# Bias of a fused adapter, router and expert layer: partial sums folded to 64 rows with high and low halves in one product, and a ScalarE copy put in another place

## What is computed

```python
# first layer, for tile b with adapter A = lora_As[itok[b]], Bm = lora_Bs[itok[b]]
y = x @ W.T + b1 + 2.0 * (x @ A) @ Bm
# second layer on y
base   = y @ base_w.T + base_b
hidden = y @ A2.T                          # 64 columns
probs  = softmax(y @ router_w.T)           # 16 experts
topw, topi = top_k(probs, 2); topw = topw / (sum(topw) + 1e-6)
delta  = sum over the two experts e of topw[e] * hidden @ B[e].T
out    = x + base + 0.5 * delta
```

## Time and profile before

| | |
|---|---|
| median of 3 runs | 101.2 us (101.11 to 102.17) |
| the profiled execution | 101.23 us |
| its span, first to last instruction | 99.4 us |
| TensorE busy | 95.7 us, 96% of the span |
| VectorE, ScalarE, GpSimd busy | 67%, 42%, 22% |
| chain that ended last | 93% TensorE, 3% transfers, 0% VectorE and ScalarE |

### The profile page before, as it was taken

The page is one execution under the profiler, slowest core; times in us unless marked ns, Lnnn a source line. Parts: engine busy times, 40 slices in busy tenths (PEclk is TensorE's granted clock), DMA queues, the critical chain, the costliest instruction groups (busy, mean ns, idle before and its releaser), DMA issues.

```text
span 99.4 us, 1810 instructions
## 1 busy us (share of the span) xinstructions
PE 95.7 (96%) x572; PEld 87.2 (88%) x572; DVE 66.1 (67%) x183; ACT 41.8 (42%) x102; POOL 22.2 (22%) x34
## 2 busy tenths in 40 slices
PE   6899999999999999999999999999999999999990
PEld 6799999999999999998898799888787887878980
DVE  5669995997475885998977577257949275572101
ACT  3615526968787545756422610451424022040000
POOL 4100004325999965109122000000000000000000
PEclk9999999999999999999999999999999999999999
DMA  2999569899457786882590736416307465020211
GB/s 37 356 364 391 174 125 377 265 366 361 121 91 191 196 257 142 229 233 47 175 300 25 206 127 178 138 35 196 109 20 199 134 170 147 0 105 0 105 59 53
DMA packets 8379, 16.91 MB, mean 170 GB/s; under 512 B 1507, under 2 KB 4067, under 8 KB 8370
## 3 DMA queue, kind: packets, MB, share of 16 engines
q1 hardware_dynamic: 7762, 16.41, 54.5%
q10 hardware_dynamic: 576, 0.39, 1.2%
q0 software_dynamic: 32, 0.00, 0.0%
HBM read 13.28 MB, written 2.16 MB: 155 GB/s over the span
## 4 chain that ended last, share of the span: by engine, by line
PE 93%; DMA 3%; DVE 0%; ACT 0%; issue 0%
PE pair L819 90%; DMA w_raw_all<-w_cat 3%; PE pair L964 1%; PE pair L966 1%; PE pair L984 1%; DVE xn L813 0%; ACT w_hi_all L421 0%; PE pair L954 0%; PE pair L943 0%; PE pair L941 0%; PE pair L933 0%
## 5 line engine op out<-in xcount | busy, mean ns | idle before, releaser
L819 PE MATMUL pair<-e_hi,w_hi_all 128*128 128x512 f32 (+1 forms) x72 | 27.1, 376 | 0.0
L819 PE MATMUL pair<-e_hi,w_lo_all 128*128 128x512 f32 (+1 forms) x72 | 26.7, 370 | 0.0
L819 PE MATMUL pair<-e_lo,w_hi_all 128*128 128x512 f32 (+1 forms) x72 | 26.7, 370 | 0.0
L536 ACT ACTIVATE w_hi_all<-exp_raw_all 128x512 fp32r<-128x512 f32 x16 | 9.7, 630 | 15.3 <-DVE exp_raw_all L754 15.3
L819 PEld LDWEIGHTS pair<-e_hi,w_lo_all 128*128 128x128 f32 x72 | 13.5, 188 | 2.5
L819 PEld LDWEIGHTS pair<-e_hi,w_hi_all 128*128 128x128 f32 x72 | 13.6, 188 | 2.5
L819 PEld LDWEIGHTS pair<-e_lo,w_hi_all 128*128 128x128 f32 x72 | 13.6, 189 | 2.0
L761 DVE TENSOR_TENSOR w_lo_all<-exp_raw_all,w_hi_all 128x512 fp32r<-128x512 f32 x16 | 10.4, 688 | 4.5 <-ACT w_hi_all L536 3.9
L754 DVE TENSOR_TENSOR exp_raw_all<-w_raw_all 128x512 f32<-128x512 f32 x16 | 11.1, 735 | 0.2 <-DMA w_raw_all<-spill 0.2
L768 DVE TENSOR_TENSOR xn<-pair,xn 128x512 f32<-128x512 f32 x7 | 4.8, 690 | 9.1 <-PE pair L819 9.1
L819 PE MATMUL pair<-p_hi,x_hi 128*128 128x304 f32 x32 | 10.0, 311 | 0.0
(11 more groups left out here) (108 smaller groups left out, 162.5 us busy)
## 6 DMA issues: line engine op xcount, KB each, us to landing
w_raw_all<-spill SPq DMA_DIRECT2D x16, 256.0 KB, 4.0
...
```

The costliest lines, as they stand in the source:

```text
L536: nc.scalar.activation(gt_hi[:, t % 2, js, :], g[:, js, :], ACT.Copy).then_inc(gh_done, 1)
L819: return nc.tensor.matmul(out_ap, lhs, rhs, start=first, stop=last)
```

## The change

1. The bias is summed over 64 rows. `bias_up`, 64x592, takes ScalarE's copy of the lower 64 rows of `bias_part`; VectorE adds the upper 64 rows to it. The rounded high part goes to rows 0 to 63 of one tile `bp_split`, the low part to rows 64 to 127, and two matmuls with the ones sum both at once, in place of four.
2. `bias_part_of(2)` moves ahead of `folded_lo(0)` on VectorE. On ScalarE the copy to `bias_up` stands ahead of `c_hi`.
3. The x copy of the third tile (`x_hi_part(2)`) moves ahead of the last `folded_hi`, with waits for its input and for the end of the folding.
4. The low part of the first tile's adapter rows is a VectorE copy from `c_lo` in place of the subtraction from PSUM; it waits for `cl_done` in place of `first_high`. `x_first(1)` no longer waits for `first_low`.

```diff
--- before.py
+++ after.py
@@ -95,8 +95,10 @@
         c_hi = sb("c_hi", [P, W2N], F32R)
         c_lo = sb("c_lo", [P, W2N], F32R)
         bias_part = sb("bias_part", [P, W2N])
-        bp_hi = sb("bp_hi", [P, W2N], F32R)
-        bp_lo = sb("bp_lo", [P, W2N], F32R)
+
+        bias_up = sb("bias_up", [P // 2, W2N])
+
+        bp_split = sb("bp_split", [P, W2N], F32R)
         bias_hi = sb("bias_hi", [FT, W2N], F32R)
         low_row = sb("low_row", [FT, 1])
         c_stack = sb("c_stack", [FT, NT, W2N], F32R)
@@ -207,6 +209,8 @@
         ch_done = sem("ch_done")
         cl_done = sem("cl_done")
         bias_step = sem("bias_step")
+        bias_moved = sem("bias_moved")
+        bias_added = sem("bias_added")
         bph_done = sem("bph_done")
         bpl_done = sem("bpl_done")
         pe_bias = sem("pe_bias")
@@ -458,16 +462,21 @@
             nc.scalar.activation(lb_hi[:, :, :].rearrange("p k (t r) -> p t k r", t=NT),
                                  lora_raw[:, :, KC * R:AL].rearrange("p t (k r) -> p t k r", k=KC),
                                  ACT.Copy).then_inc(lbh_done, 1)
-            for n in range(KC):
+            for n in range(KC - 1):
                 folded_hi(n)
+
             act.wait_ge(in_xt[1], 16)
+            act.wait_ge(pe_p, KC)
             x_hi_part(2)
+            folded_hi(KC - 1)
             x_hi_part(3)
             split_experts(0)
+            act.wait_ge(bias_step, KC)
+            nc.scalar.activation(bias_up[:, :], bias_part[P // 2:, :], ACT.Copy).then_inc(bias_moved, 1)
             act.wait_ge(pe_c, 1)
             nc.scalar.activation(c_hi[:, :], w2_cols(ps_c), ACT.Copy).then_inc(ch_done, 1)
-            act.wait_ge(bias_step, KC)
-            nc.scalar.activation(bp_hi[:, :], bias_part[:, :], ACT.Copy).then_inc(bph_done, 1)
+            act.wait_ge(bias_added, 1)
+            nc.scalar.activation(bp_split[0:P // 2, :], bias_up[:, :], ACT.Copy).then_inc(bph_done, 1)
             def lora_first():
                 z = z_lora[0]
                 act.wait_ge(pe_first, 1)
@@ -655,6 +664,7 @@
             x_lo_early(1)
             bias_part_of(0)
             bias_part_of(1)
+            bias_part_of(2)
             folded_lo(0)
             folded_lo(1)
             dve.wait_ge(lbh_done, 1)
@@ -664,13 +674,15 @@
                                     ALU.subtract).then_inc(lbl_done, 1)
             folded_lo(2)
             folded_lo(3)
-            bias_part_of(2)
             bias_part_of(3)
+            dve.wait_ge(bias_moved, 1)
+            nc.vector.tensor_tensor(bias_up[:, :], bias_part[0:P // 2, :], bias_up[:, :],
+                                    ALU.add).then_inc(bias_added, 1)
             dve.wait_ge(ch_done, 1)
             nc.vector.tensor_tensor(c_lo[:, :], w2_cols(ps_c), c_hi[:, :].bitcast(F32),
                                     ALU.subtract).then_inc(cl_done, 1)
             dve.wait_ge(bph_done, 1)
-            nc.vector.tensor_tensor(bp_lo[:, :], bias_part[:, :], bp_hi[:, :].bitcast(F32),
+            nc.vector.tensor_tensor(bp_split[P // 2:, :], bias_up[:, :], bp_split[0:P // 2, :].bitcast(F32),
                                     ALU.subtract).then_inc(bpl_done, 1)
 
             def lora_first_lo():
@@ -769,9 +781,8 @@
 
             lora_first_lo()
             dve.wait_ge(first_set, 2)
-            dve.wait_ge(first_high, 1)
-            nc.vector.tensor_tensor(c_first[F_LOW:F_LOW + R, :], w2_cols(ps_c)[0:R, :],
-                                    c_first[0:R, :].bitcast(F32), ALU.subtract).then_inc(first_low, 1)
+            dve.wait_ge(cl_done, 1)
+            nc.vector.tensor_copy(c_first[F_LOW:F_LOW + R, :], c_lo[0:R, :]).then_inc(first_low, 1)
             stack_bias()
             lora_lo(1)
             read_z(0)
@@ -896,7 +907,6 @@
                     pe.wait_ge(acc_done, t - 1)
                 elif t == 1:
                     pe.wait_ge(cl_done, 1)
-                    pe.wait_ge(first_low, 1)
                 out_cols, cols = first_half[t % 2]
                 x_side(t, out_cols, cols).then_inc(pe_first, 1)
 
@@ -922,8 +932,7 @@
                 pe.wait_ge(consts, 4)
                 pe.wait_ge(bph_done, 1)
                 pe.wait_ge(bpl_done, 1)
-                halves(ps_b, BANK - W2H, W2H, ones[:, :], bp_hi[:, :], True, False)
-                halves(ps_b, BANK - W2H, W2H, ones[:, :], bp_lo[:, :], False, True).then_inc(pe_bias, 1)
+                halves(ps_b, BANK - W2H, W2H, ones[:, :], bp_split[:, :], True, True).then_inc(pe_bias, 1)
 
             def lora_first_transpose():
                 pe.wait_ge(hh_done, 1)
```

## The result

| | before | changed |
|---|---|---|
| median of 22 runs each | 101.38 us (100.87 to 102.63) | 102.25 us (101.23 to 103.71) |
| the profiled execution | 101.23 us | 102.19 us |
| its span | 99.4 us | 100.3 us |
| TensorE busy | 95.7 us, x572 | 96.6 us, x570 |

The changed kernel takes 1.0059 times as long, with a 95% interval of 1.0035 to 1.0083: +0.6 us, at least 0.35 and at most 0.84. That is a loss, and less than 1%. (The ratio leaves out disturbed runs and agrees with the quotient of the means of the others, 102.07 and 101.47 us; the medians lie 0.87 us apart.) The forecast, no change and slightly on the slow side, had the side and the size class right and the number too low: 101.5 us, at most 101.8.

What follows compares the result with a forecast made beforehand. TensorE, without a gap from 4.3 us, bounds the kernel. -0.27 (two matmuls) + 0.04 (bias) + 0.52 (wait at `x_first(4)`) = +0.3 us on the profiled 101.23 gives 101.5 us; own range 101.3 to 101.8, with rivals 100.9 to 101.8.

Steps and rivals of the forecast that it cites:

- What bounds the kernel, and the slack: TensorE has no gap from 4.3 us on; GpSimd's tile 4 low part ends 0.36 us before TensorE loads `x_first(4)`.
- The two matmuls, -0.27: On TensorE, two of the four bias matmuls go, saving 0.27 us, all of it on the path.
- ScalarE's order and the bias steps: Earlier x copy on ScalarE gets GpSimd out of VectorE's way: 1.3 us gained ahead of the bias chain.
- The bias chain: Four links between ScalarE and VectorE after the last bias step end 0.22 us later; TensorE waits 0.04 us.
- The copy: VectorE's adapter low-row copy takes 0.46 us, goes first and costs GpSimd's tile 3 0.27 us.
- GpSimd is first: Rival, 0.24 with the copy blocking nobody: copy ends about 25.4, bias rows just in time; +0.0 to +0.1, 101.3 us.
- VectorE's `e_lo` goes first, then the cast: VectorE's waiting `e_lo` precedes GpSimd's cast; tile 4 ends at 36.41 in place of 35.84, TensorE waits until 36.44.
- The sum: Whole kernel: -0.27 (matmuls) + 0.04 (bias) + 0.52 (wait at `x_first(4)`) = +0.3 us, 101.5 us.
- how the numbers follow: Chances and range: forecast 0.46, 100.9 to 101.8 us over the cases; within 1% 0.96, slower 0.03, faster 0.01.
- The saving stays: Rival, chance 0.26: GpSimd's slack at `x_first(4)` covers the delay and most of the saving; 101.0 to 101.1 us.
- the bias chain ends after 24.0: Sign against the forecast: VectorE's low part of the bias ends after 24.0, so TensorE would wait there first.
- GpSimd's tile 3 of 1.6 us: Expected sign: GpSimd's tile 3 lasts about 1.6 us in place of 1.29 if the copy holds the ports.

Runs made afterwards that it cites:

- e8: The kernel before without the two matmuls of the bias's low part; ratio to the kernel before 1.0002 (0.9960 to 1.0044).
- e16: The kernel before with only ScalarE's x copy of the third tile moved ahead of the last `folded_hi`; ratio to the kernel before 1.0007 (0.9978 to 1.0035).
- e9: Changed kernel, VectorE's third-quarter `e_lo` one tile later, `bias_up` copy on VectorE, GpSimd's tile 3 waiting for `first_low`; ratio to the kernel before 0.9974 (0.9936 to 1.0012).
- e4: The changed kernel with ScalarE's old order, all four `folded_hi` ahead of the x copy; ratio to the kernel before 1.0056 (1.0014 to 1.0097).
- e5: The changed kernel once more, unaltered; ratio to the kernel before 1.0055 (1.0021 to 1.0088).
- e1: The changed kernel with VectorE's `e_lo` of the third quarter moved behind `route(2)`; ratio to the kernel before 0.9985 (0.9953 to 1.0017).

## Why the forecast was right in its mechanism and low in its number

**What bounds the kernel, and the slack.** Right. TensorE has no gap, so edits count only as TensorE's own work or as a wait. The slack of 0.36 us at `x_first(4)` was the number that decided: e8 uses it up with the faster TensorE, the changed kernel overdraws it. One reading of it was incomplete: the queue "without a gap" holds a hidden wait, the adapter's low part behind VectorE's `e_lo`, so tile 4 followed VectorE and not GpSimd's own start (e16).

**The two matmuls, -0.27.** Right. The product comes 0.28 us earlier in e8, the end 0.24; e9 keeps 0.30.

**ScalarE's order and the bias steps.** Right in kind: e4 puts the chain at x0 + 3.31 against 2.98. The x copy started 0.28 us after the third `p_hi` had ended, by its row for its transfer (in e5 0.22 us, by its row for TensorE), where I had 0.15 us, so everything behind it was about 0.1 late.

**The bias chain.** Forecast x0 + 2.88, measured 2.98 and 2.92. TensorE came 0.15 and 0.09 us later to the ones, not 0.04. As the forecast said, this doesn't add to the wait behind it. The four links are as long as forecast, 64 rows as long as 128 (0.77 in 22.03 and 23.57, 0.78 in the earlier trace rows).

**The copy.** This step failed in its order. I let the copy go first and hold GpSimd for 0.27 us. GpSimd came first (24.42, copy 24.57), because its own hand-over of 0.08 us is shorter than the adapter's small step of 0.20 on VectorE. So GpSimd's tile 3 lasted 1.29 us, not 1.56, and the copy 1.45, not 0.46. The rival "GpSimd is first" described this, and its price was nothing, since it took the two bias rows to be just in time. In fact they started at 26.05, and the product loaded at 27.01, 0.25 us after the load ahead of it, where loads here follow each other by 0.14, so that TensorE lost about 0.1 us. GpSimd paid too: its next cast (25.64), which met the copy, took 0.48 us in place of 0.24. That this 0.24 is nearly the 0.27 that the wrong order had charged to tile 3 is luck, and the forecast of what follows rests on it: GpSimd's last `e_lo` ended at x0 + 12.84 against the forecast 12.75.

**VectorE's `e_lo` goes first, then the cast.** Right: 1.07 us from GpSimd's end to VectorE's, as forecast; tile 4 ended at x0 + 15.67 and 15.60 against 15.59; TensorE loaded at 15.72 and 15.65 against 15.62. e1 takes this one mechanism away, and the loss in the stretch with it.

**The sum.** Right for the stretch: forecast +0.3, measured +0.34 and +0.28 at the end (76.81 and 76.75 against 76.47). Its wait at `x_first(4)` was 0.42 and 0.41 us where it had 0.52, its wait at the bias 0.15 and 0.09 where it had 0.04.

**The number.** The steps that failed are the sum's base and the range behind it ("how the numbers follow"). I added +0.3 to the profiled 101.23 as if nothing outside the rows could move, and allowed 0.1 us for what runs differ. The time outside the span, which no row shows, was put at no change without a reason, and the runs showed 0.2 us more of it. The base itself was 0.15 us low: 22 runs of the kernel before gave 101.38. Of the ratio's 0.6 us (0.35 to 0.84), 0.31 in the stretch and 0.2 outside the span make 0.5; the rest is smaller than the interval. Of the 0.75 us by which the median of 102.25 lies above 101.5, the base and the time outside the span make 0.35. The other 0.4 lies in the span of those 22 runs, whose median is 100.3 us (99.95 in e5, the same kernel). Only one of the 22 is profiled, with x0 0.54 us late, so the start is the likely place, but that isn't shown. What makes the time outside the span longer stays open too.

**The rivals.** "The saving stays" was wrong: its 0.09 us of slack was what e8 used. The sign "the bias chain ends after 24.0" came by its letter (24.34), but counted from x0 it is 2.98, which is 23.80 on the forecast's time; GpSimd's tile 3 of 1.6 us didn't come. "The copy blocks nobody, or GpSimd is first" had the order right and the end wrong. The clock did not fall at the wait of 0.42 us: from there to the last addition it takes 61.09 us (76.81 - 15.72), and before 61.09 as well (76.47 - 15.38).
